# Cross-attention loop: key projections between the value projections, and the maximum split on the vector engine

## The reference

```python
x = layernorm(x + self_attention(x))              # one head, causal
q, k, v = x @ wq, ctx @ wk, ctx @ wv              # ctx: (32, 1500, 128)
scores = einsum('bhtd,bhsd->bhts', q, k) + bias   # relative-position bias, no scale
attn = einsum('bhts,bhsd->bhtd', softmax(scores), v)
x = layernorm(x + attn @ wo)
x = layernorm(x + ffn(x))                         # two 512-wide gated layers, two 512-wide GELU layers, back to 128
```

## Time and profile before

| | |
|---|---|
| Median of 3 runs | 1085.17 us (1084.59 to 1091.04) |
| The profiled execution | 1093.1 us, its span 1091.3 |
| Mean granted TensorE clock | 0.952 |
| Busy share of the span | PE 89%, PEld 60%, DVE 66%, ACT 55%, POOL 39% |
| Turns 1 to 28 of the loop | 170.82 to 865.45 us |

### The profile page before, as it was taken

How to read it: one execution, slowest core, us unless ns; L and a number is a source line. 1 busy time by engine, 2 the same in 40 slices (tenths; PEclk the granted TensorE clock), 3 DMA queues, 4 the chain that set the end, 5 groups by cost and what they waited for, 6 DMA issues and landing times. The chain is left out here.

```text
span 1091.3 us, 25611 instructions
## 1 busy us (share of the span) xinstructions
PE 969.3 (89%) x10410; PEld 657.2 (60%) x10410; DVE 721.8 (66%) x1510; ACT 605.5 (55%) x1071; POOL 421.6 (39%) x418
## 2 busy tenths in 40 slices
PE   6754579999999999999999999989999988799996
PEld 3542256666666666666666666666666666545564
DVE  6565447878778877878778878876777774540014
ACT  2321157666667666666666666666666656352232
POOL 7330535554444555554444555554444400000000
PEclk9866689999999999999999999998999999899999
DMA  7507665555666655555665755554665420300000
GB/s 228 192 10 163 117 190 178 164 177 178 191 177 204 185 176 179 163 178 178 191 194 161 209 179 177 164 179 147 188 181 162 137 78 2 109 1 1 1 9 25
DMA packets 57388, 156.10 MB, mean 143 GB/s; under 512 B 23936, under 2 KB 36152, under 8 KB 54200
## 3 DMA queue, kind: packets, MB, share of 16 engines
q1 hardware_dynamic: 56744, 152.85, 48.1%
q10 hardware_dynamic: 528, 1.63, 0.4%
HBM read 111.63 MB, written 42.63 MB: 141 GB/s over the span
## 5 line engine op out<-in xcount | busy, mean ns | idle before, releaser
L769 ACT ACTIVATE e_sb<-st_ps 128x896 f32<-128x896 f32 (+1 forms) x384 | 354.1, 925 | 153.0 <-DVE st_ps L714 93.5
L108 DVE TENSOR_REDUCE cmax<-max_ps 112x1 f32<-112x512 f32 x512 | 337.6, 683 | 150.5 <-PE max_ps L98 150.4
L98 PE MATMUL max_ps<-kst,qst 111*112 111x512 bf16 x760 | 283.8, 401 | 37.8 <-PEq L117 14.1
L611 PEld LDWEIGHTS st_ps<-qst,kst 114*128 114x128 bf16 (+1 forms) x3072 | 191.7, 101 | 88.7 <-issue 41.8
L821 POOL TENSOR_TENSOR kpart<-k_left,kpart 128x500 bf16<-128x500 f32 x90 | 102.7, 1141 | 352.4 <-ACT k_left L787 347.8
L611 PE MATMUL st_ps<-qst,kst 114*128 114x112 bf16 (+1 forms) x3072 | 215.7, 213 | 19.5 <-DMA qst<-nmp 18.3
L105 DVE CUSTOM_DVE_ANT_0 near_out<-max_ps,near_nat 112x476 bf16<-112x476 f32 x248 | 154.0, 649 | 26.4 <-PE max_ps L98 26.4
L98 PEld LDWEIGHTS max_ps<-kst,qst 111*112 111x112 bf16 x760 | 92.2, 130 | 106.8 <-DVE cmax L108 38.9
L641 PE MATMUL pv_ps<-e_sb,vals 128*32 128x168 f32 (+1 forms) x3072 | 150.0, 313 | 0.3 <-ACT e_sb L769 0.3
L685 PEld LDWEIGHTS misc<-wv,ctxt 128*128 128x128 f32 (+1 forms) x768 | 99.6, 193 | 15.8 <-ACT vals L754 11.8
L641 PEld LDWEIGHTS pv_ps<-e_sb,vals 128*32 128x32 f32 (+1 forms) x3072 | 80.4, 109 | 47.1 <-issue 34.6
(11 more groups left out here) (127 smaller groups left out, 941.1 us busy)
## 6 DMA issues: line engine op xcount, KB each, us to landing
kst<-kparts SPq DMA_DIRECT2D x192, 375.0 KB, 6.2
kparts<-kpart SPq DMA_DIRECT2D x90, 375.0 KB, 2.7
ctxt<-in_ctxT SPq DMA_DIRECT2D x32, 750.0 KB, 7.4
qst<-qslots SPq DMA_DIRECT2D x192, 28.0 KB, 6.4
qslots<-qst SPq DMA_DIRECT2D x4, 672.0 KB, 11.2
kparts<-kst SPq DMA_DIRECT2D x6, 375.0 KB, 3.1
h<-in_h SPq DMA_DIRECT2D x2, 1024.0 KB, 8.6
qst<-nmp SPq DMA_DIRECT2D x96, 1.8 KB
```

The costliest lines, as they stand in the source:

```text
L98: return nc.tensor.matmul(dst[0:TT, 0:hi - lo], m.qst[0:M_ROW, r, p, :], m.kst[0:M_ROW, r, p, lo:hi], start=True, stop=True)
L108: return nc.vector.tensor_reduce(m.cmax[:, r, c, p:p + 1], src[0:TT, 0:BOUND[c + 1] - BOUND[c]], AX.X, ALU.max)
L611: mm = nc.tensor.matmul(st_ps[0:K, j % 2, p // 4, (p % 4) * TT:(p % 4 + 1) * TT], m.kst[0:AUG, u % RING, p, j * P:j * P + K], m.qst[0:AUG, ...
L769: nc.scalar.activation(e_sb[0:K, j % E_RING, :].rearrange("p (a c) -> p a c", a=2), st_ps[0:K, j % 2, :, 0:HALF], ACT.Exp).then_inc(s_ex, 1)
```

## The change

- The tables: the key thirds move from steps 4, 5, 6 to 1, 3, 5; the value thirds from 0, 1, 2 to 0, 2, 4; the denominators from step 3 to 6. In the head the key thirds are at 1, 3, 5. The reciprocals move from steps 4 and 5 to 6 and 7, the output product from 9 to 10.
- The maximum is split in three bf16 parts on VectorE before it is transposed (`nm3`), by four instructions, each of which waits for the one before. The three parts are transposed by one bf16 matmul with a bf16 unit matrix (`ident_b`), copied once by ScalarE, and sent to the three rows of `qst` by one transfer. The POOL chain and two of three transfers are gone.
- ScalarE's copy of `x_sb` at step 1 comes after that step's user of `misc`. POOL's three `split_k` stand one behind the other, ahead of the mask of the reciprocals.
- There is still one bank for `misc`.

```diff
--- before.py
+++ after.py
@@ -503,9 +503,8 @@
 
         k_left, kpart = sb("k_left", [C, S]), sb("kpart", [C, 3, S], BF16)
         e_sb = sb("e_sb", [P, E_RING, HT])
-        nmax = sb("nmax", [TT, PAIRS])
-
-        nmp, nm_left = sb("nmp", [PAIRS, 3, TT], BF16), sb("nm_left", [PAIRS, TT])
+        nmax, nm_left = sb("nmax", [TT, PAIRS]), sb("nm_left", [TT, PAIRS])
+        nm3, nmp, ident_b = sb("nm3", [TT, 3, PAIRS], BF16), sb("nmp", [3 * PAIRS, TT], BF16), sb("ident_b", [TT, TT], BF16)
         x_sb, den, rec = sb("x_sb", [P, PIECES * T]), sb("den", [P, PIECES * T]), sb("rec", [P, PIECES * T])
         own, x_own = sb("own", [P, PIECES]), sb("x_own", [P, PIECES * T])
         max_ps = ctx.enter_context(nc.psum_tensor("max_ps", [P, 2, 512], F32))
@@ -523,7 +522,7 @@
 
         s_kf, s_ve, s_ex, s_xr, s_nr, s_dr = (sem(n) for n in ("kf", "ve", "ex", "xr", "nr", "dr"))
 
-        s_kr, s_k3, s_np, s_ro = sem("kr"), sem("k3"), sem("np"), sem("ro")
+        s_kr, s_k3, s_ro, s_n0, s_n1, s_n2, s_ib = (sem(n) for n in ("kr", "k3", "ro", "n0", "n1", "n2", "ib"))
 
 
         s_nb, s_nm, s_rc, s_xo, s_xh, s_kz = (sem(n) for n in ("nb", "nm", "rc", "xo", "xh", "kz"))
@@ -565,11 +564,11 @@
         M0 = ST - HEAD_START // 2
         CHUNKS = PAIRS * NCH
         PAIRED = ST // 2
-        HEAD_MISC = {4: ("k", 0, 3), 5: ("k", 1, 3), 6: ("k", 2, 3), M0: ("nmt", 0, 1),
+        HEAD_MISC = {1: ("k", 0, 3), 3: ("k", 1, 3), 5: ("k", 2, 3), M0: ("nmt", 0, 1),
                      9: ("v", 0, 1), 10: ("v", 1, 1), 11: ("v", 2, 1)}
-        MISC = {0: ("v", 0, 1), 1: ("v", 1, 1), 2: ("v", 2, 1), 3: ("den", 0, -1),
-                4: ("k", 0, 3), 5: ("k", 1, 3), 6: ("k", 2, 3), M0: ("nmt", 0, 1)}
-        NM, REC_A, REC_B, XH = M0 - 1, 4, 5, 9
+        MISC = {0: ("v", 0, 1), 1: ("k", 0, 3), 2: ("v", 1, 1), 3: ("k", 1, 3), 4: ("v", 2, 1), 5: ("k", 2, 3),
+                6: ("den", 0, -1), M0: ("nmt", 0, 1)}
+        NM, REC_A, REC_B, XH = M0 - 1, 6, 7, 10
 
         def max_items(g, u, j):
 
@@ -604,7 +603,7 @@
             def scores(g, u, j):
 
                 if j == 0:
-                    pe.wait_ge(s_md[u % 2], filled(g, u, 2, 48))
+                    pe.wait_ge(s_md[u % 2], filled(g, u, 2, 16))
                 wait(pe, s_ex, batch(g, u) * ST + j - 1)
                 K = st_rows(j)
                 for p in range(PAIRS):
@@ -693,7 +692,9 @@
                                          x_sb[:, A_COLS:A_COLS + B_COLS], start=True, stop=True).then_inc(s_dn, 1)
                     if kind == "nmt":
                         pe.wait_ge(s_nm, n + 1)
-                        nc.tensor.transpose(misc[0:PAIRS, 0:TT], nmax[:, :], m.ident[0:TT, 0:TT]).then_inc(s_nt, 1)
+                        pe.wait_ge(s_ib, 1)
+                        nc.tensor.matmul(misc[0:3 * PAIRS, 0:TT], nm3[:, :, :].rearrange("q i p -> q (i p)"),
+                                         ident_b[:, :], start=True, stop=True).then_inc(s_nt, 1)
 
             run(iteration)(pe)
 
@@ -721,8 +722,17 @@
                     if j == NM and live(g, u + 1):
                         dve.wait_ge(s_mr, (b + 2) * CHUNKS)
                         wait(dve, s_nt, b + 1)
+                        wait(dve, s_nm, b + 1)
                         nc.vector.tensor_reduce(nmax[:, :], m.cmax[:, (u + 1) % 2, :, :].rearrange("q c p -> q p c"),
-                                                AX.X, ALU.max, negate=True).then_inc(s_nm, 1)
+                                                AX.X, ALU.max, negate=True).then_inc(s_n0, 1)
+                        dve.wait_ge(s_n0, b + 2)
+                        nc.vector.tensor_copy(nm3[:, 0, :], nmax[:, :]).then_inc(s_n1, 1)
+                        dve.wait_ge(s_n1, 2 * b + 3)
+                        nc.vector.tensor_tensor(nm_left[:, :], nmax[:, :], nm3[:, 0, :], ALU.subtract).then_inc(s_n1, 1)
+                        dve.wait_ge(s_n1, 2 * b + 4)
+                        nc.vector.tensor_copy(nm3[:, 1, :], nm_left[:, :]).then_inc(s_n2, 1)
+                        dve.wait_ge(s_n2, b + 2)
+                        nc.vector.tensor_tensor(nm3[:, 2, :], nm_left[:, :], nm3[:, 1, :], ALU.subtract).then_inc(s_nm, 1)
                     if live(g, u - 1):
                         if j == REC_A:
                             dve.wait_ge(s_dr, b)
@@ -768,10 +778,6 @@
                         K = st_rows(j)
                         nc.scalar.activation(e_sb[0:K, j % E_RING, :].rearrange("p (a c) -> p a c", a=2),
                                              st_ps[0:K, j % 2, :, 0:HALF], ACT.Exp).then_inc(s_ex, 1)
-                    if j == 1 and live(g, u - 1):
-                        act.wait_ge(s_pv, b * PAIRED)
-                        wait(act, s_xo, b - 1)
-                        nc.scalar.copy(x_sb[:, :], pv_ps[:, 0:PIECES * T]).then_inc(s_xr, 1)
                     user = misc_user(g, u, j)
                     if user:
                         kind, part, lag = user
@@ -793,9 +799,12 @@
                         if kind == "nmt":
                             act.wait_ge(s_nt, n + 1)
                             if live(g, u):
-                                act.wait_ge(s_md[u % 2], filled(g, u, 2, 48))
-                            nc.scalar.copy(nmp[:, 0, :], misc[0:PAIRS, 0:TT])
-                            nc.scalar.copy(nm_left[:, :], misc[0:PAIRS, 0:TT]).then_inc(s_nr, 1)
+                                act.wait_ge(s_md[u % 2], filled(g, u, 2, 16))
+                            nc.scalar.copy(nmp[:, :], misc[0:3 * PAIRS, 0:TT]).then_inc(s_nr, 1)
+                    if j == 1 and live(g, u - 1):
+                        act.wait_ge(s_pv, b * PAIRED)
+                        wait(act, s_xo, b - 1)
+                        nc.scalar.copy(x_sb[:, :], pv_ps[:, 0:PIECES * T]).then_inc(s_xr, 1)
 
             run(iteration)(act)
 
@@ -806,6 +815,7 @@
             for h in range(2):
                 ins = nc.gpsimd.memset(m.kst[:, SA_K, h * PAIRS // 2:(h + 1) * PAIRS // 2, :], 1.0)
                 ins.then_inc(s_kz, 1)
+            nc.gpsimd.tensor_copy(ident_b[:, :], m.ident[0:TT, 0:TT]).then_inc(s_ib, 1)
             pool.wait_ge(s_own, 16)
 
             def split_k(g, u, c):
@@ -830,6 +840,8 @@
             def iteration(g, u):
                 b = batch(g, u)
                 split_k(g, u, 0)
+                split_k(g, u, 1)
+                split_k(g, u, 2)
                 if live(g, u - 1):
                     pool.wait_ge(s_rc, 2 * b)
                     nc.gpsimd.tensor_tensor(rec[:, :].rearrange("p (i t) -> p i t", t=T),
@@ -837,20 +849,6 @@
                                             own[:, :].unsqueeze(2).broadcast_to([P, PIECES, T]),
                                             ALU.mult).then_inc(s_ro, 1)
                     pool.wait_ge(s_ro, b)
-                split_k(g, u, 1)
-                if live(g, u + 1):
-                    done = 3 * (b + 1)
-                    pool.wait_ge(s_nr, b + 2)
-                    nc.gpsimd.tensor_tensor(nmp[:, 1, :], nm_left[:, :], nmp[:, 0, :],
-                                            ALU.subtract).then_inc(s_np, 1)
-                    pool.wait_ge(s_np, done + 1)
-                    nc.gpsimd.tensor_tensor(nm_left[:, :], nm_left[:, :], nmp[:, 0, :],
-                                            ALU.subtract).then_inc(s_np, 1)
-                    pool.wait_ge(s_np, done + 2)
-                    nc.gpsimd.tensor_tensor(nmp[:, 2, :], nm_left[:, :], nmp[:, 1, :],
-                                            ALU.subtract).then_inc(s_np, 1)
-                    pool.wait_ge(s_np, done + 3)
-                split_k(g, u, 2)
 
             run(iteration)(pool)
 
@@ -882,10 +880,9 @@
                     sp.wait_ge(s_kf, 3 * (u + 4 - SA_K))
                     store_k(u + 3, 0)
                 if live(g, u + 1):
-                    sp.wait_ge(s_np, 3 * (b + 2))
-                    for i in range(3):
-                        sp.dma_start(m.qst[M_ROW + i:M_ROW + i + 1, (u + 1) % RING, :, :],
-                                     nmp[:, i, :]).then_inc(s_md[(u + 1) % 2], 16)
+                    sp.wait_ge(s_nr, b + 2)
+                    sp.dma_start(m.qst[M_ROW:AUG, (u + 1) % RING, :, :],
+                                 nmp[:, :]).then_inc(s_md[(u + 1) % 2], 16)
                 if later(g, u + 3):
                     sp.wait_ge(s_kr, 6 * (u + 4 - SA_K) - 1)
                     store_k(u + 3, 1)
```

## The result

The changed kernel took 1173.65 us (median of 4 runs, 1169.35 to 1174.48) against 1087.73 for the kernel before on the same chip: a ratio of 1.078, 95% interval 1.073 to 1.083. Slower, as forecast; the forecast of 1159 was 15 us low. The profiled run of the changed kernel was its shortest, 1169.35, with a span of 1167.6, 76.3 over the 1091.3 of before.

What follows compares the result with a forecast made beforehand. A turn was taken as paced by TensorE's program order and its waits. Halves of 15.0 and 12.2 made 27.2 us a turn: +67 over 28 turns, -1 at head and tail, from 1093.1 to 1159 us; 8-in-10 range 1105 to 1180.

Steps and rivals of the forecast that it cites:

- Banks: Steps 2, 4 and 6 each wait 0.58 us for the misc bank behind a key part; net +0.96 a turn.
- Denominator and reciprocals: Step 6: VectorE stands still 0.35 us for the denominator, so step 7's reductions run from 3.55 to 4.85.
- The chain: Step 8: five dependent VectorE instructions take 1.06 us against 0.18, holding TensorE's transposing matmul.
- Second reciprocal: End of VectorE's step 7: delays step 9's first chunk to 1.27 us after step start, against 0.39; second half 12.2.
- One transfer: Turn's end: one copy and transfer bring the maximum's rows early; the 0.37 us wait goes, 0.33 returns at step 0.
- the long waits: Rare waits for the maximum's rows, longest 2.52 us, then a lower clock: 8.9 us in all, expected to vanish.
- 28 turns: 761.6: Term for the full turns of the loop, each taken as 27.2 us: 761.6 against 694.6, +67.
- the ends: Outside the full turns: head +2, turn 0 +1, turns 29 and 30 minus 1.0 and 2.8; together -1 us.
- The gaps absorb it: Rival: VectorE's idle 5.1 us a turn hides the added work; turn 24.1, 1072 us; chance 0.07.
- banks only: Rival: chain and reciprocals hidden, only the misc bank waits cost; turn 25.1, 1100 us; chance 0.07.
- The second reciprocal absorbed: Rival: bank waits and split chain cost, but step 9 absorbs the second reciprocal; turn 26.1, 1128 us; chance 0.14.
- The clock rival: Rival: waits at steps 8 and 9 drop the clock every turn, at most 3.2 us each; 1249 us; chance 0.05.

Runs made afterwards that it cites:

- split_only: The changed kernel with the old tables, old x_sb copy place and old POOL order, leaving only VectorE's split and the single transfer: 1196.76 us, ratio 1.096.
- order_only: The kernel before with the new tables, late x_sb copy and POOL's key splits together; POOL chain and three transfers stay: 1137.76 us, ratio 1.042.
- split_pool_later: VectorE split and single transfer in the kernel before's order, with POOL's second split_k waiting until the split is done: 1104.60 us, ratio 1.017.
- no_second_reciprocal: The changed kernel without the second reciprocals (L741), so POOL's mask waits for the first alone: 1157.95 us, ratio 1.066.
- no_second_copy: The changed kernel without ScalarE's second copy of each key part (k_left): 1134.96 us, ratio 1.040.
- transposed_at_9: The changed kernel with the matmul that transposes the maximum at step 9 in place of 8: 1188.69 us, ratio 1.088.
- value_part_late: The kernel before with value parts at steps 0, 2 and 10 and the context loaded after the maximum's rows: 1114.75 us, ratio 1.026.
- no_vector_split: The changed kernel with the maximum written once as bf16 and the four split instructions left out: 1132.47 us, ratio 1.037.

## Why the prediction came out as it did

**Banks: right.** Three waits behind key parts, 0.8 each in the waits view; steps 2 and 4 last 2.30 as step 6 did in the kernel before (2.25 to step 7 in the earlier trace rows). The first half of the turn was to be 15.0 and is 14.88 (504.89 to 519.77), and step 6 was to be 1.85 and is 1.91.

**Denominator and reciprocals: right.** VectorE was to stand 0.35 for the denominator; it stood 0.42. Step 7's reductions were to end 4.85 after step 6 began; they ended at 524.64, that is 4.87.

**The chain: right, by an estimate that leaned on one row.** Five small instructions 0.20 to 0.22 apart, 1.00 in all where 1.06 was reckoned. A link lasts 0.17, and starts 0.20 to 0.22 after the last and not at the bound of 0.10, so here a wait on the same engine costs the whole duration and 0.03 to 0.05. The 0.07 that I took from the Trainium skill's "VectorE: DVE Perf Modes", section "The TRN2 errata", is not what these instructions show; the section itself calls that row too low for a single instruction and gives about 150 cycles as the fixed part, which makes 0.17 at 8 elements (an estimate from its 0.96 GHz). So I read the page wrong: by its measured figure nothing comes off the sum. What I didn't see either is that the price holds only while POOL is quiet. In the changed kernel POOL is clear 0.2 us ahead of the first cast; in POOL's old order two of the four instructions are held (split_only). The sum was right by luck in this: nothing in it says that POOL must be clear. In the head, which has its own order, the collision is in the changed kernel too; the three held instructions end 0.02 to 0.03 after POOL's (132.02, 133.11, 134.33):

```profile
131.26 0.79 DVE L729 CAST nm<-nmax 112x8 bf16<-112x8 f32 x1
...
132.08 1.05 DVE L731 TENSOR_TENSOR nm_left<-nmax,nm 112x8 f32<-112x8 f32 x1
...
133.37 0.98 DVE L735 TENSOR_TENSOR nm<-nm_left,nm 112x8 bf16<-112x8 f32 x1
```

**Second reciprocal: right in kind, 0.2 too dear.** Step 9's first chunk was to start 1.27 after the step and started at 1.09 (525.91 to 527.00). The second half came out at 12.05 instead of 12.2.

**One transfer: right in the sum, wrong in the cause.** The waits for `nmp` are gone and step 0 went from 1.73 to 2.07, the 0.33 foreseen. But I put the gain down to the single transfer, and order_only loses the landing wait with three: the longer turn is what gives the rows time. Of the long waits order_only keeps one, of 1.4 us. The 8.9 us of the long waits did not stay saved.

**What the sum left out: the clock.** I gave the clock a rival's place only, at one fall each turn, and the forecast had none. It fell in 6 of the 28 turns, for 765.60 - 28 x 26.93 = 11.6 us, 1.2 or 2.3 a fall. The step that was short is "28 turns: 761.6": it takes every turn for an ordinary one. It took the two falls of the kernel before for gone with the long waits, and put none in their place. That the turns came to 765.6, only 4 more, is luck in part, since the turn's own error (26.93 for 27.2) gave 7.6 back. The rest of the 10.3 between 1159 and the profiled 1169.35 is the ends: turn 0 cost 4.0 where I took 1, turns 29 and 30 gave 1.9 less than I took, the end 1.1 more. These terms I had guessed from their bounds rather than worked out by steps.

**How much waiting brings a fall** is not settled. At steps 8 and 9 of every turn TensorE waits in each run as follows; the falls are those in the 28 turns.

| Run | Waits at steps 8 and 9, us | Falls |
|---|---|---|
| order_only | 0.53 | 0 |
| split_pool_later | 0.66 | 0 |
| no_second_reciprocal | 0.92 | 5 |
| changed kernel | 0.67 and 0.52 | 6 |
| no_second_copy | 0.67 and 0.52 | 9 |
| transposed_at_9 | 1.51 | 21 |
| split_only | 2.40 | 26 |

value_part_late, whose wait for the stacked transfers is about 1.5 on the mean, had 10, and no_second_copy has more falls than the changed kernel with the same two waits in a shorter turn, so their length alone doesn't decide. In the changed kernel all six falls come 21.8 to 22.0 us into their turn, within the second wait; the 22 other turns have the same two waits and no fall. What tells the turns apart no run shows. In the kernel before each of the two falls goes with one wait for the rows: of 2.52, within which the first began (at 736.8; the wait ended at 737.45), and of 1.64, right behind it. No run made one wait longer with all else kept. The Trainium skill's "TensorE: Matmul & The Clock Gate", section "A second HAM failure mode: psum-queue depth-cycling", tells of a kernel whose clock swung because TensorE paused briefly and often between groups of matmuls; these runs agree with it in that one wait of 0.92, or one of 0.67 and one of 0.52, coming back every turn, went with falls. Also open is why the other runs of the changed kernel took up to 5 us longer than the profiled one: their mean granted clock was 0.936 to 0.938 against its 0.940, which fits more falls, but no trace shows them.

**The rivals.** "The gaps absorb it" and "banks only" needed the chain hidden; no_vector_split shows all 0.82 that the split adds paid. "The second reciprocal absorbed" fell with no_second_reciprocal: its step 9 is 0.70 shorter. The clock rival came true in about a fifth of the turns, at 1.2 or 2.3 instead of 3.2.

## What to carry to other kernels

Before moving small work onto VectorE, look at what POOL runs at that moment: 8 elements cost 1 us in split_only, and a wait on POOL cured it. The same holds for an experiment: one that leaves work out can let another engine's work come sooner and collide. When transfers are late, first try to send each piece when it is ready; that gave 1% here, where shifting the split to VectorE lost 1.7% at its best (split_pool_later) and 10% at its worst (split_only). And an edit that turns waits into other waits on TensorE should be sized with the clock in mind, by turns and not by the steady turn alone.

## What the runs showed of the hardware

- VectorE's casts and subtractions of 8 elements in SBUF take 0.17 alone, and up to 1.06 when they begin while a POOL instruction of 1.13 runs (split_only); in no_second_reciprocal the cast took 0.42 beside a POOL instruction of 0.66. They end with it. A cast that began 0.07 before POOL's instruction kept its 0.17. The cast has one SBUF input and was held like the subtraction. The other way round, a POOL subtraction of 1.13 took 1.43 when a VectorE product of 0.44 had begun 0.02 before it, in all 28 such cases of split_only (1.42 to 1.43). VectorE's reductions out of PSUM kept their 0.65 to 0.69 in the same stretches.
- The granted clock fell to 1.2 GHz at TensorE waits of 0.5 to 2.4 us that came back every turn: 6 falls in 28 turns with two of 0.67 and 0.52, 5 with one of 0.92 (no_second_reciprocal), 21 with one of 1.51 (transposed_at_9), 26 with one of 2.40 (split_only), none with one of 0.66 (split_pool_later).
- The waits view can call a wait "issue" when the releaser is a small instruction of VectorE (L696).
